# A transformer layer on one core: three first stack copies on ScalarE's queue, a third projection moved behind the loop, score banks lent earlier

## The reference

```python
h = layernorm(x)
q, k, v = h @ Wq + bq, h @ Wk + bk, h @ Wv + bv           # split into 16 heads
scores = q @ k.T / sqrt(16) + slope[head] * distance[key]  # ALiBi; causal mask
x = x + softmax(scores) @ v @ Wo + bo
h = layernorm(x)
x = x + bitlinear(sigmoid(bitlinear(h, w1)) * bitlinear(h, w2), w3)
# bitlinear(a, w) = a @ T.T,  T = clip(round(w / mean|w|), -1, 1)
```

## Time and profile before

| | us |
|---|---|
| three timed runs | 706.96 (median), 3025.71, 625.81 |
| the profiled execution | 623.65 |
| its span, first to last instruction | 621.6 |
| TensorE busy | 588.2 (95%) |
| VectorE busy | 465.2 (75%) |
| ScalarE busy | 364.0 (59%) |
| mean granted TensorE clock | 0.995 of full speed |

### The profile page before, as it was taken

One profiled execution on the slowest core, in us unless ns is written; L12 is line 12 of the kernel. 1 busy time (PEld: TensorE's weight loads), 2 busy tenths in 40 slices (PEclk: granted clock), 3 DMA queues, 4 the chain that ended last, 5 costly groups with the idle time before them and its releaser, 6 DMA issues.

```text
span 621.6 us, 10829 instructions
## 1 busy us (share of the span) xinstructions
PE 588.2 (95%) x3452; PEld 365.0 (59%) x3452; DVE 465.2 (75%) x1206; ACT 364.0 (59%) x779; POOL 184.3 (30%) x394
## 2 busy tenths in 40 slices
PE   7888889999999999999999999999999999999987
PEld 5565456565656565555566666556456555566487
DVE  5978988577878876578787788888788788712187
ACT  3446447655654547567475456477577576587721
POOL 7646522261342241340212422203200210242500
PEclk9999999999999999999999999999999999999999
DMA  6896743652313116423130131155141130011000
GB/s 192 266 277 153 213 122 88 206 152 74 87 37 97 44 35 196 148 76 85 37 101 22 37 104 35 53 143 155 36 122 36 36 89 1 1 46 45 1 18 34
DMA packets 27452, 57.50 MB, mean 93 GB/s; under 512 B 5316, under 2 KB 14916, under 8 KB 23940
## 3 DMA queue, kind: packets, MB, share of 16 engines
q1 hardware_dynamic: 27396, 56.82, 32.4%
HBM read 40.69 MB, written 14.80 MB: 89 GB/s over the span
## 4 chain that ended last, share of the span: by engine, by line
PE 75%; DVE 16%; issue 4%; ACT 2%; POOL 1%; DMA 1%; ACTq 0%; POOLq 0%; DVEq 0%
PE pO L1165 19%; PE pS L1146 19%; PE pM L1126 16%; PE pM L1101 5%; DVE pm L1335 5%; DVE pM L1338 3%; PE pM L1034 3%; PE pM L1109 3%; PE pM L1087 2%; PE pM L1042 2%; PE pS L1034 1%; PE pM L1146 1%; ACT probs L949 1%; PE pS L1101 1%; DVE work L1303 1%
## 5 line engine op out<-in xcount | busy, mean ns | idle before, releaser
L949 ACT ACTIVATE probs<-pS 128x512 f32<-128x512 f32 (+3 forms) x615 | 289.6, 545 | 161.2 <-PE pS L1146 159.2
L1335 DVE TENSOR_REDUCE pm<-pM 128x1 f32<-128x512 f32 x384 | 239.1, 681 | 42.9 <-PE pM L1126 42.2
L1146 PE MATMUL pS<-qst,kst 128*128 128x512 f32 (+3 forms) x615 | 235.1, 400 | 4.7 <-ACT probs L949 2.4
L1126 PE MATMUL pM<-kst,qst 126*128 126x512 f32 (+3 forms) x640 | 228.8, 386 | 10.7 <-DVE pm L1338 3.9
L1146 PEld LDWEIGHTS pS<-qst,kst 128*128 128x128 f32 x615 | 114.6, 190 | 83.9 <-issue 44.3
L1126 PEld LDWEIGHTS pM<-kst,qst 126*128 126x128 f32 x640 | 120.1, 191 | 52.0 <-DVE pm L1335 15.1
L1338 DVE CUSTOM_DVE_ANT_0 pM<-pM,mask 128x128 f32<-128x128 f32 (+3 forms) x256 | 119.7, 523 | 35.8 <-PE pM L1126 35.5
L827 POOL TENSOR_SCALAR_AFFINE_SELECT probs<-probs 128x128 f32<-128x128 f32 x256 | 76.3, 310 | 215.9 <-ACT probs L949 208.5
L1165 PE MATMUL pO<-probs,vals 128*17 128x512 f32 (+3 forms) x1264 | 132.9, 538 | 0.0
L1165 PEld LDWEIGHTS pO<-probs,vals 128*17 128x17 f32 x1264 | 29.6, 97 | 64.5 <-issue 39.4
L816 POOL CAST hT<-work 128x256 fp32r<-128x256 f32 (+1 forms) x34 | 13.6, 399 | 86.1 <-DVE work L1303 78.8
(11 more groups left out here) (157 smaller groups left out, 414.0 us busy)
## 6 DMA issues: line engine op xcount, KB each, us to landing
kst<-parts SPq DMA_DIRECT2D x78, 256.0 KB
qst<-parts SPq DMA_DIRECT2D x30, 256.0 KB, 4.0
parts<-qk_hl SPq DMA_DIRECT2D x28, 256.0 KB, 4.3
ctx_dram<-ctx_raw SPq DMA_DIRECT2D x15, 256.0 KB, 3.7
xin<-in_L_attn_x SPq DMA_DIRECT2D x5, 512.0 KB, 4.9
out<-work SPq DMA_DIRECT2D x8, 256.0 KB, 4.3
work<-ctx_dram SPq DMA_DIRECT2D x7, 256.0 KB
work<-rden_dram SPq DMA_DIRECT2D x7, 256.0 KB
```

The lines of the kernel that those rows point to most:

```text
L949: nc.scalar.activation(probs[:, n % PSLOTS, q0:CH], score(n)[:, q0:CH], ACT.Exp)\
L1126: pe.matmul(max_bank(x)[:, 0:N], qst[0:R_MAX, u % QSLOTS, h, t * P:(t + 1) * P], kst[0:R_MAX, n % KSLOTS, h, 0:N], start=True, stop=True). ...
L1146: pe.matmul(score(n)[:, q0:CH], kst[0:R_END, sl, h, b:b + P], qst[0:R_END, u % QSLOTS, h, q0:CH], start=True, stop=True).then_inc(scores_r ...
L1335: nc.vector.tensor_reduce(dst, bank, AX.X, ALU.max).then_inc(max_free, 1)
```

## The change

- `first_half` on SyncE's queue keeps one of the two copies of k's high half, both of k's low half and both of q's low half. The other three (one of k's high half, both of q's high half) are issued by ScalarE right after the activation that makes the half. ScalarE waits for the fills of the first key and query stack before its head activations.
- Wk and Wq have a semaphore each.
- VectorE fills one key stack before the statistics of x, and the other behind its ALiBi and constant work, ahead of its first split.
- `bv_w` is made by ScalarE, behind `size_of_weights(0)`.
- GpSimd waits for the first negated maxima before it splits k of chunk 1.
- `swap_max(0)` comes ahead of the second half of the q projection; `KEEP_WARM` is 8.
- The exchange of unit 1 is met after part 0 of its step instead of part 2.
- The lent banks start from the step behind the last turn (141) instead of step 144; the last exchange takes a bank of the ring of two.
- Three `up` groups are late. In the tail the order is: wo half 0, late 1, wo half 1, late 2, x2T, down. GpSimd splits late 2 between its two last powers.

```diff
-    late = [("up", NCH - 2, 1, FT - 2), ("up", NCH - 2, 1, FT - 1), ("down", NCH - 2, 1)]
+    late = [("up", NCH - 2, 1, m) for m in range(FT - 3, FT)] + [("down", NCH - 2, 1)]
...
+    swap_in = {(first_step[1] - 2, 0) if u == 1 else at: u for at, u in swap_in.items()}
...
-    WARM_UP, KEEP_WARM = 30, 12
+    WARM_UP, KEEP_WARM = 30, 8
...
-    tail_groups = [("ctxT", 0), ("ctxB", 0), ("ctxT", 1), late[0], post[0], ("ctxB", 1), late[1], *post[1:3], late[2], *post[3:]]
-    tail_on_vector = [("ctxT", 0), ("ctxT", 1), late[0], post[0], late[1], post[2], post[1], late[2], *post[3:]]
+    tail_groups = [("ctxT", 0), ("ctxB", 0), ("ctxT", 1), late[0], post[0], ("ctxB", 1), late[1], post[1], late[2], post[2], late[3], *post[3:]]
+    tail_on_vector = [("ctxT", 0), ("ctxT", 1), late[0], post[0], late[1], late[2], post[2], post[1], late[3], *post[3:]]
...
-    lent_from = 1 + max(i for i, use in enumerate(ring_use) if use[0] == "swap")
+    lent_from = 1 + max(i for i, use in enumerate(ring_use) if use[0] == "turn")
+    LENT_FROM = 1 + max(t for t in range(NS) if step_turns[t])
...
-        m = n - G * first_step[NU - 1]
+        m = n - G * LENT_FROM
...
-            first_half(("k", 0, 0), 0)
+            first_half(("k", 0, 0), 0, [1])
+            first_half(("k", 0, 0), 1)
             sp.wait_ge(al_out, 32)
             alibi_rows(0)
-            first_half(("k", 0, 0), 1)
             sp.wait_ge(q_rows, 1)
-            first_half(("q", 0, 0), 0)
             first_half(("q", 0, 0), 1)
...
+                pool.wait_ge(lo_ok, i)
...
+            pool.wait_ge(nm_ok, 1)
             split_lo(K10)
...
-            for h in range(2):
-                power(powers + 1 + h, 2 * h, 2 * h + 2)
+            power(powers + 1, 0, 2)
+            split_hidden(late[2])
+            power(powers + 2, 2, 4)
...
-            act.wait_ge(wqk_in, 32)
-            for dst, src, scale in ((wk_s, w_raw[0], 1.0), (wq_s, w_raw[1], HD ** -0.5)):
+            for i, dst, src, scale in ((0, wk_s, w_raw[0], 1.0), (1, wq_s, w_raw[1], HD ** -0.5)):
+                act.wait_ge(wqk_in[i], 16)
...
-            for g in head_first[KT:KT + len(head_splits)]:
+            act.wait_ge(k_rows, 1)
+            act.wait_ge(q_rows, 1)
+            for g in head_splits:
                 side_op(g)
+                for b in range(2) if g == ("q", 0, 0) else range(1) if g == ("k", 0, 0) else ():
+                    act.wait_ge(head_hi, split_no[g] + 1)
+                    dst, src = first_rows(g, 0, b)
+                    nc.scalar.dma_start(dst, src).then_inc(k_in[0] if g[0] == "k" else q_in[0], 16)
             side_op(("v", 0, 0))
             size_of_weights(0)
+            act.wait_ge(bv_in, 16 * KT)
+            act.wait_ge(const_ok, 1)
+            for m in range(KT):
+                ins = nc.scalar.activation(bv_w[:, m, :], ones, ACT.Identity, scale=bv_c[:, m:m + 1])
+            ins.then_inc(bv_ok, 1)
...
-            side_group(Q10, 1)
             swap_max(0)
+            side_group(Q10, 1)
...
-            for n in range(KPOOL, KSLOTS):
+            def key_rows(n):
+
                 nc.vector.memset(kst[:, n, :, :].bitcast(F32), 1.0).then_inc(k_rows_v, 1)
+
+            key_rows(KPOOL)
             dve.wait_ge(x_in, 16)
...
             nc.vector.memset(vals[:, 0:T // P // 2, :, HD:VW], 1.0).then_inc(rows_ok, 1)
+            for n in range(KPOOL + 1, KSLOTS):
+                key_rows(n)
...
-            dve.wait_ge(bv_in, 16 * KT)
             dve.wait_ge(const_ok, 1)
-            for m in range(KT):
-                ins = nc.vector.tensor_scalar(bv_w[:, m, :], ones, bv_c[:, m:m + 1], None, ALU.mult)
-            ins.then_inc(bv_ok, 1)
...
-                if g in late[1:]:
-                    h = int(g == late[2])
+                if g in (late[1], late[3]):
+                    h = int(g == late[3])
...
-                if g[0] == "up":
+                if g[0] == "up" and g != late[2]:
                     split_hidden(g)
```

More of the change, by code:

```diff
@@ L363, in preln_layer @@
         x_in = sem("x_in")
-        wqk_in = sem("wqk_in")
+        wqk_in = [sem(f"w{n}_in") for n in "kq"]
         bias_in = sem("bias_in")
@@ L488, in need_empty, with first_rows @@
             eng.wait_ge(side_a if e == "a" else side_v, n)
+        def first_rows(g, part, b):
+            row = b * P // 2 + part if g[0] == "k" else part * P // 2 + b
+            end = row // (P // 2) * (P // 2) + R_HALF
+            stack = kst if g[0] == "k" else qst
+            return stack[row:end:2, 0, :, :].bitcast(F32), hi_lo(split_no[g])[0:G * HD, part, :]
         @block.sync
@@ L556, in load_q, with first_half @@
                                  src.to_broadcast([HD, 2, G * CH])).then_inc(q_in[v % QSLOTS], 16)
-            def first_half(g, part):
-                i = split_no[g]
+            def first_half(g, part, stripes=range(2)):
                 if part == 0:
-                    sp.wait_ge(head_hi, i + 1)
+                    sp.wait_ge(head_hi, split_no[g] + 1)
                 else:
                     need_split(sp, g)
-                src = hi_lo(i)[0:G * HD, part, :]
-                for b in range(2):
-                    row = b * P // 2 + part if g[0] == "k" else part * P // 2 + b
-                    end = row // (P // 2) * (P // 2) + R_HALF
-                    if g[0] == "k":
-                        sp.dma_start(kst[row:end:2, 0, :, :].bitcast(F32), src).then_inc(k_in[0], 16)
-                    else:
-                        sp.dma_start(qst[row:end:2, 0, :, :].bitcast(F32), src).then_inc(q_in[0], 16)
+                for b in stripes:
+                    dst, src = first_rows(g, part, b)
+                    sp.dma_start(dst, src).then_inc(k_in[0] if g[0] == "k" else q_in[0], 16)
             def alibi_rows(n):
@@ L636, in _ @@
             load_x(0)
-            for dst, src in ((w_raw[0], Wk), (w_raw[1], Wq)):
-                sp.dma_start(dst, src.rearrange("(k p) n -> p k n", p=P)).then_inc(wqk_in, 16)
+            for i, src in enumerate((Wk, Wq)):
+                sp.dma_start(w_raw[i], src.rearrange("(k p) n -> p k n", p=P)).then_inc(wqk_in[i], 16)
             sp.dma_start(al[:, 0, :], alibi).then_inc(al_in, 16)
@@ L1178, in _ @@
                     side_group(*head_between[k])
+            swap_max(0)
             side_group(Q10, 1)
-            swap_max(0)
             pe.wait_ge(rows_ok, 1)
```

## The result

The changed kernel takes 619.32 us (the median of four executions: 619.02, 619.30 and 619.34, and one of 3023.02 that, like the 706.96 and 3025.71 of the kernel before, was disturbed and says nothing of the kernel). The ratio to the kernel before is 0.9922, 95% interval 0.9895 to 0.9949. Run once more in ten executions beside nineteen of the kernel before, its median was 621.10 against 624.10, ratio 0.9945 [0.9927, 0.9962]: 3.0 us less. The base of the forecast, 623.65, holds: in four later sets the kernel before has medians of 623.48 to 624.10. The profiled execution took 619.34 us with a span of 617.6, against 623.65 and 621.6: 4.0 us less span.

A forecast was written before the change was run, and what follows sets the result against it. TensorE, busy 588.2 of 621.6 us, was taken to bound the kernel, with its idle time at the ends. The terms -2.5 - 0.4 - 0.3 - 0.9 = -4.1 us took 623.65 to 619.5 us; range 616.8 to 624.8.

The forecast's parts named there:

- Step a: Head, start of the statistics of x: one key stack fill ahead instead of two starts them 0.6 us earlier.
- Step b: Head, first stack copies: with three issues off SyncE's queue, first max matmul at 19.5 instead of 21.76 us, 2.25 earlier.
- Rival 1: First stack copies land no earlier because all queues share what moves them; 621.7 us in all, chance 0.15.
- Step c: Head, wide copy of bv moved to ScalarE: VectorE ready for maxima at 20.5, last maximum at 28.9 instead of 31.39.
- Step d: Head, last maximum to first score: POOL's wait saves 0.5 us at the negation; first score at 33.4 against 35.95.
- The head: Everything up to the first scores: 2.5 us less, bounds 0.4 to 3.3 less.
- Part 2: Earlier exchange of unit 1's maxima, 48 to 51 us: the 0.69 us wait goes; 0.4 us less, bounds -0.7 to +0.7.
- rival 3: The early exchange of unit 1 blocks TensorE, with copies landing no earlier too: slower, 625.3 us, chance 0.08.
- Part 3: Banks lent three steps earlier, steps 141 to 143: 0.3 us less, bounds 0 and -0.6.
- Part 4: Projection moved from step 154 to the tail, where idle time covers it: 0.9 us less, bounds 0 and -1.0.
- Rival 4: More than forecast: the exchange decides the first score and the statistics start at their best; 618.0 us, chance 0.07.

The follow-up runs named there:

- bv_vector: The changed kernel with the wide copy of bv made by VectorE again instead of ScalarE; 620.41 us, ratio 0.9943 to the kernel before.
- pool_free: The changed kernel without GpSimd's wait for the first negated maxima; 621.42 us, ratio 0.9955 to the kernel before.
- swap1_old: The changed kernel with the exchange of unit 1 put back to its old, later place in the step; 619.59 us, ratio 0.9937 to the kernel before.
- the control: The changed kernel run again without any edit; 621.10 us, ratio 0.9945 to the kernel before.
- warm_two: The changed kernel with twelve dummy transposes in TensorE's gap at 71.8 us and six more in the gap ahead; 617.33 us, ratio 0.9898 to the kernel before.
- lent_old: The changed kernel with the banks lent from step 144 on, as before; 621.00 us, ratio 0.9956 to the kernel before.
- warm_mid: The changed kernel with twelve dummy transposes in TensorE's idle gap at 71.8 us; 618.56 us, ratio 0.9917 to the kernel before.

## Why the prediction was right in the sum and wrong in its terms

**Step a held**: 0.6 earlier, as taken.

**Step b failed** at "such a copy lands in 2.6 us". That held for one queue issuing one copy after the other. The last issue came nearly as forecast, 16.90 against 16.6, and the v projection ended at 19.5 as forecast; but the copy took 3.85 us and landed at 20.75 and not at 19.2, so the first max matmul came at 20.84 and not at 19.5. Rival 1 had the mechanism, half of it: its condition was that the copies land no earlier, and they landed 0.6 earlier than from one queue. The Trainium skill (DMA: Bandwidth & Descriptors, "Issuing engines are not separate DMA queues") says that a second issuing engine saves issuing time only. I turned it into "by it I lose nothing", because I counted 1.9 us of issuing as saved. The trace agrees with the page, and the saving was smaller still: of 2.0 us by which the last issue was earlier, 1.4 were taken back in moving, at 0.95 busy DMA engines. I had read the 0.94 of 20 to 24 us, and not asked what the stretch in question would look like with the same bytes in less time. ScalarE's side held: its longest issue took 1.06 and not 0.62 to 0.76, the activation of the second k projection started at 16.84, and VectorE still came to its split only at 17.71.

**Step c held in kind, not in size**: 0.75 instead of most of 2.5. The lock is there, as the Trainium skill has it (SBUF — State Buffer, "SBUF: two separate sides"): in bv_vector the two instructions take 2.19 us under GpSimd's fill, against 0.68 on ScalarE. The first maximum is held only behind them (1.49 us); in the changed kernel it takes 0.30 in the middle of the same fill (20.72 to 22.52), so the case in which a fill holds every VectorE instruction did not occur. But TensorE came to its first turn only at 20.84, so VectorE's readiness at 20.5 could not be used.

**Step d held in kind.** The instruction went from 0.67 to 0.17. From negated maxima to score 3.9 us were forecast, and it took 34.24 - 30.49 = 3.75. By pool_free, though, the wait put in for it is worth nothing that can be read off: the half microsecond is paid back, as I had said of 0.4. That the half q projection "hides under" the exchange holds only as long as GpSimd waits too; in pool_free it is what ScalarE waits for. The head came to 1.5 instead of 2.5. Undone one at a time, the queue is worth 0.6 and bv 0.75, each give or take 0.3. These shares need not add up, and the other edits of the head were not undone alone: the moved fill, the order of `swap_max(0)`, the semaphores of Wk and Wq, and the eight transposes instead of twelve, of which the traces show that from the start of the transposes to the first score it is 0.82 us instead of 1.33. The 35.95 from which I counted was the modelled end of the transposes; the first score starts at 35.78 in the same trace.

**Part 2 failed** at "so the wait of 0.69 goes". It went, and TensorE then waited for GpSimd, whose zeroing stood behind a fill. In the kernel before, the two waits lay over each other. I had priced what stood behind TensorE's new wait and not looked at who is next late when the old one goes. It measured 0.0 against 0.4, with a scatter of 0.2; rival 3, the slower one, did not occur: TensorE stood 1.41 us at the exchange, the weighted sums behind it came 0.4 later than in swap1_old (45.61 against 45.21), and at the exchange of unit 2 nothing of that was left.

**Part 3 failed** at the bound "0 and -0.6", taken from TensorE's idle time in 540 to 550 us. It gave 1.3. A matmul that waits for its bank can be drawn as busy: the bound from idle time was none. From the first to the third of the weighted sums below, TensorE is drawn busy for 10.19 us and idle for 0.62 before, and busy for 9.14 and idle for 0.34 with five banks; so 1.05 of the gain lay in what was drawn as busy. What measures it is the pace of the work: the weighted sums that start 5.37 and 5.44 us apart before (537.26, 542.63, 548.07) start 4.48 and 5.00 apart with five banks (535.50, 539.98, 544.98).

**Part 4 held**: 0.95, with the tail paying nothing. The cover was the x2T gap (1.02 to 0.40) and ScalarE followed TensorE.

Head and part 2 were 1.5 us too high (2.9 forecast, a lead of 1.4 at the exchange of unit 2), part 3 was 1.0 too low, and the lead grew by 0.4 in the middle, which no experiment traces to an edit. A forecast of 4.1 against 4.0 is therefore luck: errors that cancel.

Two of the prediction's bounds don't follow from its terms. Rival 4's 618.0 takes all four parts at their best, -5.6, though it names two steps of the head; and the -6.2 of the range's low end is 0.6 below that without a reason. The two per cent that I took for what a measurement of this kernel can tell from no change was too coarse: a change of 0.8% came out with an interval that excludes no change.

## What to carry to other kernels

Before a transfer is put on a second queue, look at the share of the DMA engines in the very stretch that it will move to; here, where that share got to 0.95, 0.6 of 2.0 us of earlier issuing arrived. Before a wait is removed, list who waits at the same place for another engine, and price the second one. Don't bound the worth of more PSUM banks by TensorE's idle time; compare the same step with fewer and more banks, and when whole runs differ by 1 to 2 us, look first at the granted clock by stretch.

## What the runs showed of the hardware that I had not expected

**The clock falls in the middle of a full kernel.** TensorE is 95% busy over the span, yet its granted clock goes to half (1.2 of 2.4 GHz) for a few microseconds at certain places: behind 70 to 75 us, where TensorE is busy 2.75 us (before) or 3.13 us (after) of 5.00, and in some executions near 92 and 214 us. In after, 211 to 214 had 1.66 of 3.00 us busy and the clock stayed at 1.00; in other executions of nearly the same work it fell. One such stretch costs, at equal points of the work, 0.5 us (90 to 95 us, the control), 1.3 us (74 to 77, warm_two) or 1.5 us (214 to 217, lent_old between units 7 and 8). The mean clock of an execution tells how much of it ran at half clock, and the time goes with it: the square of their correlation is 0.67 over the ten executions of the control and 0.78 over the nineteen of the kernel before. It does not explain all, since a stretch costs more in one place than in another: at the same mean clock of 0.994 the changed kernel took 619.3 us in its first set and 620.77 in the second. What else differs between the sets was not found. Single executions on one chip, with the mean clock of each (all four of warm_mid, some of the others):

```
changed kernel   619.08 (0.997)  619.65 (0.997)  620.77 (0.994)  621.27 (0.992)  621.79 (0.992)  623.05 (0.992)
warm_mid         617.31 (1.000)  617.75 (0.996)  619.38 (0.994)  621.27 (0.992)
kernel before    623.10 (0.994)  623.57 (0.994)  624.10 (0.994)  625.71 (0.988)  626.10 (0.988)
```

Eighteen transposes that compute nothing, in 2.4 us of idle time, were worth 2 us of 617 in the profiles, more than any edit of the change that was undone alone. That they keep the clock up rests on five of six executions with a mean clock of 0.999 or 1.000, against none of thirteen of the changed kernel and two of seven of bv_vector; that the idle time is what brings the fall is the likeliest reading, and what else decides it from one execution to the next stays open.

**Repairs in a head with 0.95 busy DMA engines collide.** Three edits that looked harmless (stores later, ALiBi rows later, a fill earlier) left the kernel 1.2 to 4.5 us behind at the exchange of unit 2, two of them through a 16 KB transfer of maxima that took 3.9 and 4.65 us (in the kernel before it was there within 2.5 us of its issue), and two with a fall of the clock during or at the end of the wait.
